# Clearing the rows behind the experts' regions from GpSimd's queue instead of SyncE's

## The reference, cut to what matters

```python
x = layernorm(x + attention(x, w_qkv, w_conv1))        # x: (2, 2048, 256)
xf = x.reshape(-1, 256)                                # T = 4096 tokens
scores = softmax(xf @ gate_w.T)                        # E = 8 experts
top_vals, top_idx = top_k(scores, 2)                   # K = 2 choices of each token
w_dense = zeros((T, 8)).at[arange(T)[:, None], top_idx].set(top_vals)
h = einsum('td,ehd->teh', xf, W1)                      # W1: (8, 384, 256)
y, g = split(h, 2, axis=-1)
eo = einsum('teh,edh->ted', y * silu(g), W2)           # W2: (8, 256, 192)
z = einsum('te,ted->td', w_dense, eo) + gated_mlp(xf, Ws1, Ws2)
out = layernorm(x + z)
```

## Time and profile before

| | us |
|---|---|
| three executions, median | 362.41 |
| lowest and highest | 361.57, 365.29 |
| profiled execution, span from first to last instruction | 354.0 |

### The profile page before, as it was taken

How to read it: one execution, slowest core, us unless ns; L and a number is a source line. 1 busy time by engine, 2 the same in 40 slices (tenths; PEclk the granted TensorE clock), 3 DMA queues, 4 the chain that set the end, 5 groups by cost and what they waited for, 6 DMA issues and landing times.

```text
span 354.0 us, 7780 instructions
## 1 busy us (share of the span) xinstructions
PE 315.3 (89%) x2225; PEld 282.8 (80%) x2225; DVE 265.5 (75%) x1037; ACT 192.7 (54%) x425; POOL 197.5 (56%) x223
## 2 busy tenths in 40 slices
PE   2879899999999989999989979999999999999700
PEld 1446788789888878888889979999999999999600
DVE  0886679866989897966686765676678886988785
ACT  1043686646657362733335644555655566868862
POOL 4048750746778858667271542444757675686620
PEclk9969999999999999999999998999999999999955
DMA  7967420212371202442124643444899797789758
GB/s 221 378 220 262 126 62 0 95 47 75 101 216 58 92 33 93 114 136 101 35 98 140 191 144 100 129 131 131 178 247 204 202 243 190 177 236 252 204 189 324
DMA packets 31383, 54.63 MB, mean 154 GB/s; under 512 B 4880, under 2 KB 22544, under 8 KB 31344
## 3 DMA queue, kind: packets, MB, share of 16 engines
q1 hardware_dynamic: 23136, 29.82, 28.1%
q0 software_dynamic: 8208, 24.32, 23.9%
HBM read 29.73 MB, written 24.40 MB: 153 GB/s over the span
## 4 chain that ended last, share of the span: by engine, by line
PE 48%; DVE 16%; DMA 12%; SPq 8%; POOL 6%; issue 4%; ACT 4%; POOLq 0%; DVEq 0%; ACTq 0%
PE bank L1062 15%; PE bank L946 10%; PE bank L1088 8%; PE bank L968 4%; DMA stage<-ws_t 4%; PE bank L931 3%; PE bank L1071 3%; DMA stage<-rows_in 3%; PE bank L1031 3%; DVE xs L1174 3%; DVE htlo L1379 2%; SPq L415 2%; DVE mix L1374 2%; POOL rows_in L560 2%; POOL w1lo L516 2%
## 5 line engine op out<-in xcount | busy, mean ns | idle before, releaser
L600 POOL DMA_INDIRECT rows_out<-stage,place x71 | 69.4, 977 | 67.2 <-ACT stage L769 51.8
L560 POOL DMA_INDIRECT rows_in<-x,slot x64 | 65.3, 1020 | 47.1 <-DVE slot L1289 30.6
L749 ACT ACTIVATE stage<-bank 128x384 f32<-128x384 f32 (+1 forms) x36 | 17.5, 486 | 43.7 <-PE bank L1062 43.7
L1062 PE MATMUL bank<-w1hi,xthi 128*128 x142 | 39.8, 362 | 1.3 <-DVE xs L1385 1.1
L769 ACT ACTIVATE stage<-bank,weight 128x256 f32<-128x256 f32 x71 | 30.0, 471 | 15.8 <-PE bank L1088 15.7
L1062 PE MATMUL bank<-w1hi,xtlo 128*128 x142 | 36.9, 341 | 0.0
L1062 PE MATMUL bank<-w1lo,xthi 128*128 x142 | 36.8, 340 | 0.0
L1391 DVE TENSOR_TENSOR xtlo<-bank,xthi 128x512 fp32r<-128x512 f32 (+1 forms) x36 | 24.3, 676 | 13.7 <-ACT xthi L695 13.4
L1519 DVE TENSOR_TENSOR stage<-bank,stage 128x384 f32<-128x384 f32 (+1 forms) x36 | 19.8, 551 | 18.6 <-ACT stage L749 18.5
L687 ACT ACTIVATE mix<-bank 128x512 f32<-128x512 f32 x24 | 14.2, 591 | 34.1 <-PE bank L946 34.1
L946 PE MATMUL bank<-xthi,ws1hi 128*128 128x512 f32 x96 | 31.3, 407 | 0.0
(11 more groups left out here) (242 smaller groups left out, 893.4 us busy)
## 6 DMA issues: line engine op xcount, KB each, us to landing
stage<-rows_in SPq DMA_DIRECT2D x71, 133.0 KB, 2.6
xs<-rows_out POOLq DMA_DIRECT2D x12, 512.0 KB, 6.5
xs<-x SPq DMA_DIRECT2D x8, 512.0 KB, 9.2
out<-xs SPq DMA_DIRECT2D x7, 512.0 KB, 5.4
stage<-w_t SPq DMA_DIRECT2D x8, 384.0 KB, 4.4
rows_in<-clear SPq DMA_DIRECT2D x16, 133.0 KB
rows_out<-stage,place POOLq DMA_INDIRECT x71, 3.3
stage<-w_t SPq DMA_DIRECT2D x2, 512.0 KB, 3.9
```

The costliest lines, as they stand in the source:

```text
L560: pool.indirect_dma_start(rows_in[0:E * CAP, :], bass.IndirectOffsetOnAxis(slot[:, q * G + t, k:k + 1], 0), x2[q % 2][:, t, :], None).then ...
L600: pool.indirect_dma_start(rows_out[:, :], bass.IndirectOffsetOnAxis(place[:, 2 * j + b:2 * j + b + 1], 0), by[j % 4][:, b * C:(b + 1) * C] ...
L749: act.activation(bsg[j % 2][:, 0:width(j)], bank_h[j % 2][:, 0:width(j), H:F], ACT.Silu).then_inc(s_bsg, 1)
L1062: mm = pe.matmul(bank_h[j % 2][:, b, 0:F], bx[j % 2][:, (2 * b + k) * P:(2 * b + k + 1) * P], w[:, bass.ds(e, 1), k, :], start=(a == 0), s ...
```

## The change

The eight writes behind the ends move from SP to GpSimd. On SP, `load_rows(4)` to `load_rows(7)` now follow each other, without the wait for `s_ends` and without two writes behind each. On GpSimd the eight writes stand between the last group's scatters and the first scatter of results; they signal a semaphore of their own, `s_past`, for which SP waits ahead of pair 8.

```diff
-        s_pad = sem("padding_written")
+        s_pad, s_past = sem("padding_written"), sem("past_regions_written")
...
-            for j in range(4):
+            for j in range(FULL // 2):
                 load_rows(j)
-            sp.wait_ge(s_ends, 1)
-            share_of = E // (FULL // 2 - 4)
-            for j in range(4, FULL // 2):
-                load_rows(j)
-                for e in range((j - 4) * share_of, (j - 3) * share_of):
-                    r = sp.value_load(zrow[0:1, e:e + 1], min_val=0, max_val=ROWS - P)
-                    sp.dma_start(rows_in[bass.ds(r, P), :], clear[:]).then_inc(s_pad, 16)
             for n in range(2):
                 sp.wait_ge(s_sc[n], 16 * K * G * NP)
-            sp.wait_ge(s_pad, 16 * (IDLE + E))
+            sp.wait_ge(s_pad, 16 * IDLE)
+            sp.wait_ge(s_past, 16 * E)
...
+            pool.wait_ge(s_ends, 1)
+            for e in range(E):
+                r = pool.value_load(zrow[0:1, e:e + 1], min_val=0, max_val=ROWS - P)
+                pool.dma_start(rows_in[bass.ds(r, P), :], clear[:]).then_inc(s_past, 16)
```

## The result

The changed kernel takes 364.32 us (median of 17 executions, 362.00 to 367.86), the kernel before, run between them, 362.41 (17 executions, 359.60 to 366.60). The ratio is 1.005, with a 95% interval of 1.0026 to 1.0074: half a per cent slower, within the 1% that the forecast called no change, and 5.7 us above the forecast of 358.6.

A forecast was written before the change was run, and what follows sets the result against it. PE, the busiest engine, was taken to bound the kernel, held by pair 8's late load behind SP's requests. Span 354.0 less 3.85 is 350.15 us, plus 8.4 around it gives 358.6; range 357.2 to 362.5.

The forecast's parts named there:

- The late load and its price: At pairs 8 and 9, PE came 2.23 us late, then lost 1.62 to a slow clock; removing this gains 3.85 us.
- released by DVE's places and not by the writes: SP's load of pair 8 would go on when DVE ends the places, near 199.6 us, the writes having landed earlier.
- With the 8.4 us around it (median less span): Added to the forecast span of 350.15 us, this gives the forecast time of 358.6 us.
- PE does not wait between 185.4 and 208 [...] so that time stands: Ahead of pair 8, PE is busy 22.60 of 22.60 us, so DVE still ends the places at 199.61.
- Cost nothing, hidden by those 16.5 us: GpSimd's result scatters start some 2.4 us late; ACT needs their buffer only four pairs, 16.5 us, later.
- the 195.8 forecast: On GpSimd, the first scatter of results would start near 195.8 us, behind the eight moved writes.
- The time of one write, w: Each of GpSimd's eight moved writes takes 1.26 us, bounded by 1.00 and 2.06; break-even at 2.11.
- Last landing 198.2: The last of GpSimd's eight writes lands at 198.2 us, ahead of the 199.6 that the places set.
- The register work does not add up: Rival: register work adds up on GpSimd, 2.06 us a write, PE still idles; gain 0.4 us, 362.0; chance 0.16.
- GpSimd does not wait for DVE: Rival: GpSimd writes its DMAs only while DVE is idle; 8.7 us more than before, 371.1; chance 0.05.
- given back further down: Rival: from 270 to 292 us transfers set the pace and loads come late; half the gain lost, 360.5; chance 0.13.
- The rule in the Trainium skill: On moving SP's requests: spreading DMAs saves only issue time, usually small; by that alone 362.4 us stays.

The follow-up runs named there:

- e6: The kernel before, with GpSimd waiting after four of the eight scatters in each of the last two groups until they have landed; 358.92 us, ratio 0.9976.
- e7: The changed kernel, with GpSimd waiting after four of the eight scatters in each of the last two groups until they have landed; 355.46 us, ratio 0.9883.
- b1: The kernel before, unchanged, run again for a second profile; 362.93 us, ratio 0.9994, span 362.5.
- b3: The kernel before, unchanged, run once more for a third profile; one execution, 361.46 us, span 359.7.
- e4: The changed kernel, with GpSimd waiting until the transposes of pair 3 are done before its eight writes; 365.14 us, ratio 1.0139 to the kernel before.
- e15: The changed kernel, with GpSimd's wait in the middle of the eight scatters in the last group alone; 358.38 us, ratio 0.9893 to the kernel before.
- e14: The changed kernel with GpSimd's wait in the middle of both last groups' scatters, measured a second time; 357.73 us, ratio 0.9887 to the kernel before.
- e9: The kernel before with all eight writes on SP ahead of pair 4's load, and GpSimd pausing after every two scatters in the last two groups; 355.47 us, ratio 0.9884.
- e5: The kernel before with all eight writes on SP ahead of pair 4's load, and the last group's scatters held until pair 2 is transposed; 361.42 us, ratio 1.0059.
- e13: The changed kernel, with GpSimd waiting until its last token scatters have landed before its first register load; 364.15 us, ratio 1.0021 to the kernel before.

## Why the prediction was wrong

**The late load and its price: right.** The step "PE does not wait, its clock does not fall, and 3.85 us are gained" came as said at its place, 4.13 and 4.11 us in place of 6.35 and 5.74, and in the median where no long standstill lies in between (e6 to e7): 3.46 us. Pair 8's load was released by DVE's places and not by the writes, also as said (209.71 and 209.74 us).

**"With the 8.4 us around it (median less span)": wrong.** Outside the span lie 1.9 us, not 8.4. The remaining 6.5 us are lost inside the span of a median execution, and the profile at hand was of one that did not have them: against it the repeat b1 reaches pair 2 at 186.00 us and not 182.57, takes 1.4 us more from there to pair 9, and 141.6 us from pair 9 to the end in place of 138.0. The prediction said how the span stands to the median and did not ask whether 8.4 us is a likely size for it. This step alone did not move the forecast, since it was added to both kernels; it hid the next.

**"PE does not wait between 185.4 and 208 [...] so that time stands": the step that failed.** It was read from the earlier trace rows for 22.60 of 22.60 us busy, and holds in the quick execution only. In the two repeats, b1 and b3, PE stands in this stretch, some 1.7 us more between pairs 2 and 3 than in the first profile, while GpSimd issues its eight scatters. The change put its register loads into that run (180.9 to 189.0 us), and the distance grew from some 6.0 to 9.87 us. That is 3.6 to 4.0 us lost, to which the prediction gave nothing. Won are the two late spacings at pairs 8 and 9: 3.75 us by those of b1, but 1.92 by those of b3, where the clock did not fall behind the wait (1.00 from 214.6 to 218.6 us; in b1 0.67 from 215.1 to 219.1). So the sum lies between no change and some 2 us slower, and the measured ratio of 1.005 (1.9 us) is inside that.

**"Cost nothing, hidden by those 16.5 us": right for those whom it named.** The first scatter of results started at 203.53, later than the 195.8 forecast, but it waited for ACT, 8.94 us after the last write. The question asked there was who waits for GpSimd's results. Nobody did; the cost was to engines that wait for each other while GpSimd works.

**The time of one write, w: outside both ends.** Forecast 1.26 us with bounds of 1.00 and 2.06; measured 0.54. The neighbours by which it was bounded, L574 at 998 ns and the scatters at 957 ns, are not near in cost. The register work ran ahead altogether. Where the register work cannot run ahead, in e4, writes start 194.21 to 203.17 us for eight, 1.28 us apart, which is the 1.26 taken.

**Last landing 198.2.** The last write starts at 194.0 and lands 3.9 us later at most, by 198.5; right by two errors, as the scatters ended 4.8 us later than in the profile of before and the writes took half the time.

**The rivals.** The register work does not add up (0.54, not 2.06 us). GpSimd does not wait for DVE: in e7 it issued six writes in 3.29 us from 188.07, while DVE was busy for 3.04 of them, which agrees with what the prediction said against this rival. Whether something was given back further down the profiles do not tell: from pair 9 to the end pass 141.1 and 143.4 us in the two profiles of the changed kernel, 141.6 and 140.9 in the two repeats of the kernel before. The way in which it did go, a cost to PE through the work that SyncE and GpSimd do beside a run of scatters, was none of the rivals.

**The rule in the Trainium skill.** The Trainium skill (DMA: Bandwidth & Descriptors, "Issuing engines are not separate DMA queues") has DMAs spread over engines save issue time alone, which is usually small. The total agrees with it, 1.005, and the reason does not: issue time was worth 3.5 us as soon as the run was cut (e6 to e7).

## What to carry to other kernels

Before a profile is used for a sum, put its span plus what lies around it (here 1.9 us) beside the measured times: if it falls below all of them, the execution is not the one that is being timed, and a stretch in which it shows no wait proves nothing. When work is moved into another engine's queue, look not only at who waits for its results but at what that engine does without a pause there: a run of eight back-to-back GpSimd DMAs was itself the critical resource, and a wait in its middle turned a change that lost 0.5% into one that wins 1.1% (e15, in the last group alone: 0.9893, 0.9837 to 0.9948; e14, in the last two: 0.9887, 0.9847 to 0.9928). The same wait without the change gained nothing that can be told from noise (e6, 0.9976, 0.9942 to 1.001). The first profile is a warning here: its run of eight was not cut, and it had no standstill.

## What the runs showed of the hardware

While GpSimd issues scatters back to back, signals from PE's finished matmuls reach DVE and ACT late: 6.5 us after the recorded end in the changed kernel (185.14 to 191.67), 1.4 us after the last of the eight scatters ended. The recorded change of that one semaphore orders all profiles in which it is recorded (all but e9). It comes 0.01 us behind the matmul in the first profile and in e5, where the run lies elsewhere; 0.1 to 0.8 us in the profiles with the cut run; 1.7 to 3.2 in b1, b3, e4 and e13; and 5.1 to 6.7 in the eight with register loads or writes in the run. Six scatters in a row, behind eight writes, did it too (e4, PE idle 4.15 us), and in e5 single pieces of PE came 1.41 and 1.42 us apart (the scatters beside them 1.27). With runs of four (e7) no wait of PE was longer than 1.03 us there.

What holds the engines is open, but it is more than signals. SyncE has a register instruction ahead of each load that waits for no semaphore and usually takes 29 ns. In the first profile of the kernel before and in the changed kernel (by tile `rows_in`; ns min/median/max, first and last start):

```profile
L416 SPq MOVE stage<-rows_in x71: 29/29/38, 144.1 to 315.4; - x71
L416 SPq MOVE stage<-rows_in x71: 4/29/708, 147.6 to 323.2; - x71
```

In each of the 19 profiles taken after the first the longest such instruction takes 468 to 718 ns, in the first 38, and such ones are spread over the second part of the program, also in those with the cut run (e7: 704). The records differ in the same way. The first profile has all 16 completion records of each of the last eight scatters, and 4474 completion records of DMAs in all; the 19 others have 2488 to 2784, again also those with the cut run. So records are missing everywhere there, and not only beside a run of scatters. The Trainium skill (DMA: Bandwidth & Descriptors, "Why a DMA increments its semaphore by 16 and not by 1") has each of the 16 DMA engines post one increment for a DMA of GpSimd; the first profile agrees. That a record is missing does not mean that its increment is: in e7 GpSimd goes on at 183.31 behind a wait for four scatters' 64 increments, of which 24 are recorded.

The quick execution is thus the one that has its records whole and no such pauses. One candidate that fits and that no run here can test is the recording itself: the Trainium skill (NOTIFIC — the notification-queue block, "Overflow: three behaviours, one of which stalls the engine") describes record queues that drop a record or stall the engine when full, and every execution timed here was one whose spans and clocks were recorded. If it is the recording, the standstill and what cutting the run gains would be less in an execution without records, or gone; such an execution would tell.

A write of 128 rows with a register for its address takes GpSimd 0.54 us (0.542 to 0.607), and its sequencer loads the registers while the engine is still at eight earlier DMAs, up to 9.3 us ahead (180.9 against 190.2 us).
